# A window-attention block with MLP on one core: finer waits and another order at the start of the MLP stage

## What is computed

```python
y = layernorm(x, g1, b1); y = roll(y, (-2, -2))
# windows of 4 x 32 = 128 tokens, 16 per image, 4 heads of 8 channels
q, k, v = split(xw @ qkv_w + qkv_b)
attn = softmax(q * SCALE @ k.T + bias + mask)
o = (attn @ v) @ proj_w + proj_b
x = x + roll(o, (2, 2))
z = layernorm(x, g2, b2)
z = gelu(z @ fc1_w + fc1_b) @ fc2_w + fc2_b      # 32 -> 128 -> 32 channels, exact Gelu
return x + z
```

## Time and profile before

| | us |
|---|---|
| median of 3 runs | 214.05 |
| lowest and highest | 213.61, 214.38 |
| the profiled execution | 213.55 |
| its span in the profile | 211.7 |
| TensorE busy | 190.5 (90%) |
| VectorE busy | 157.1 (74%) |
| ScalarE busy | 146.6 (69%) |
| GpSimd busy | 134.1 (63%) |

### The profile page before, as it was taken

How to read it: one execution, slowest core, us unless ns; L and a number is a source line. 1 busy time by engine, 2 the same in 40 slices (tenths; PEclk the granted TensorE clock), 3 DMA queues, 4 the chain that set the end, 5 groups by cost and what they waited for, 6 DMA issues and landing times.

```text
span 211.7 us, 10978 instructions
## 1 busy us (share of the span) xinstructions
PE 190.5 (90%) x4768; PEld 115.9 (55%) x4768; DVE 157.1 (74%) x221; ACT 146.6 (69%) x217; POOL 134.1 (63%) x148
## 2 busy tenths in 40 slices
PE   0789869798989999999999999999999998979884
PEld 0754534456556657656665676576567654443212
DVE  3895956675768878876987888687766977657874
ACT  7555378645868588768867895877557656588883
POOL 7786399671246995999499869844762291702730
PEclk9999979999999999999999999999999999999999
DMA  6924538656433741554365236414620000000324
GB/s 187 273 65 143 172 125 246 165 174 191 137 119 105 217 141 60 176 155 132 107 182 161 81 112 177 127 62 152 207 58 5 8 5 6 3 0 3 150 99 152
DMA packets 24296, 25.61 MB, mean 121 GB/s; under 512 B 3556, under 2 KB 21732, under 8 KB 24164
## 3 DMA queue, kind: packets, MB, share of 16 engines
q1 hardware_dynamic: 23496, 24.16, 37.3%
q10 hardware_dynamic: 752, 0.74, 1.3%
HBM read 16.24 MB, written 8.39 MB: 116 GB/s over the span
## 4 chain that ended last, share of the span: by engine, by line
PE 53%; POOL 13%; issue 13%; ACT 7%; SPq 5%; DVE 4%; DMA 3%; POOLq 0%; DVEq 0%; ACTq 0%
PE pav L992 10%; PE ps L957 9%; PE ps L972 7%; POOL rstd L403 4%; SPq L213 4%; PE ps L943 4%; PE ps L919 4%; PE ps L1010 3%; POOL parts L421 3%; PE pq L1094 3%; PE pq L880 2%; PE pq L1100 2%; ACT prob L765 2%; DMA X<-x_tok 2%; ACT q_rows L770 2%
## 5 line engine op out<-in xcount | busy, mean ns | idle before, releaser
L560 DVE TENSOR_REDUCE m_parts<-ps 128x8 f32<-128x1024 f32 x64 | 78.1, 1222 | 31.7 <-PE ps L943 31.4
L765 ACT ACTIVATE prob<-ps 128x1024 f32<-128x1024 f32 x64 | 65.5, 1024 | 34.9 <-PE ps L972 33.6
L403 POOL TENSOR_TENSOR rstd<-var,neghalf 128x16 f32<-128x16 f32 x16 | 47.4, 2963 | 8.2 <-DVE var L525 7.3
L992 PE MATMUL pav<-prob,va 128*32 128x128 f32 x1024 | 42.2, 278 | 0.2 <-issue 0.2
L957 PE MATMUL ps<-rel_j,id_b 96*32 96x512 bf16 x512 | 40.2, 380 | 2.2 <-DVE m_parts L560 0.9
L972 PEld LDWEIGHTS ps<-q_rows,k_rows 64*64 64x64 bf16 x1024 | 16.9, 106 | 27.0 <-issue 22.4
L992 PEld LDWEIGHTS pav<-prob,va 128*32 128x32 f32 x1024 | 24.8, 109 | 9.5 <-ACT prob L765 4.6
L972 PE MATMUL ps<-q_rows,k_rows 64*64 64x128 bf16 x1024 | 27.6, 224 | 1.8 <-DMA q_rows<-m_rows 1.6
L943 PEld LDWEIGHTS ps<-k_rows,q_rows 64*64 64x64 bf16 x1024 | 22.7, 108 | 6.5 <-issue 0.6
L943 PE MATMUL ps<-k_rows,q_rows 64*64 64x128 bf16 x1024 | 25.6, 217 | 0.0
L919 PE MATMUL ps<-rel_i,ident_b 64*64 64x512 bf16 x256 | 25.3, 383 | 0.0
(11 more groups left out here) (128 smaller groups left out, 309.4 us busy)
## 6 DMA issues: line engine op xcount, KB each, us to landing
slots<-parts SPq DMA_DIRECT2D x21, 256.0 KB, 3.0
q_rows<-slots SPq DMA_DIRECT2D x42, 128.0 KB
k_rows<-slots SPq DMA_DIRECT2D x40, 128.0 KB
X<-x_tok SPq DMA_DIRECT2D x8, 256.0 KB, 4.0
y_tok<-res SPq DMA_DIRECT2D x7, 256.0 KB, 2.0
q_rows<-m_rows SPq DMA_DIRECT2D x32, 8.0 KB
bias_parts<-rel_parts SPq DMA_DIRECT2D x3, 128.0 KB
slots<-parts SPq DMA_DIRECT2D x3, 128.0 KB, 3.5
```

Of the source, the lines that this page charges most:

```text
L403: pool.tensor_tensor(rstd[:, i, :], var[:, i, :], neghalf[:], ALU.pow).then_inc(rstd_done[i], 1)
L560: dve.tensor_reduce(dst, first_home(j)[:].rearrange("p (a u n) -> p a u n", u=2, n=TOK), AX.X, ALU.max, negate=True).then_inc(max_done, 1)
L765: act.activation(prob[:, j % NPROB, :], ps2[:], ACT.Exp).then_inc(exp_done, 1)
L992: mm = pe.matmul(pav[32 * h:32 * (h + 1), 128 * (j % 4):128 * (j % 4 + 1)], va[:, b % 2, at:at + 32], prob[:, j % NPROB, src:src + 128], s ...
```

## The change

`fc1` gets a parameter `halves`. The wait for older Gelus now stands ahead of each half: half h of image m waits for 2m + h - 2 finished Gelu halves (0 or less is no wait). The waits that only guard the first call stand as before. At the start of the end stage, half 0 of `fc1(1)` stands ahead of `tokens_first(15)`, half 1 behind it; `fc1(2)` and `project_out(15)` stand ahead of `fc2(0)`, which `fc2(1)` follows directly. On VectorE, `add_attention(15)` stands ahead of `mlp_tokens(0)`.

```diff
--- before.py
+++ after.py
@@ -698,8 +698,8 @@
             copy_oT(OCTETS - 1)
             normalize(OCTETS - 1)
             copy_onT(OCTETS - 1)
+            add_attention(OCTETS - 1)
             mlp_tokens(0)
-            add_attention(OCTETS - 1)
             dve.wait_ge(x2_done, OCTETS)
             means(second_norm(B - 1), B - 1)
             center(second_norm(B - 1), B - 1)
@@ -994,23 +994,23 @@
                                        start=wi == 0, stop=wi == 1)
                 mm.then_inc(av_done, 1)
 
-            def fc1(m):
-                pe.wait_ge(yT2_done, m + 1)
+            def fc1(m, halves=(0, 1)):
+                if 0 in halves:
+                    pe.wait_ge(yT2_done, m + 1)
                 if m == 0:
                     pe.wait_ge(max_done, PAIRS)
                     pe.wait_ge(mrow_done, GROUPS)
                     pe.wait_ge(va_done, B)
                     pe.wait_ge(x2_done, OCTETS - 2)
-                else:
-                    pe.wait_ge(gelu_done, 2 * m - 1)
-                if m == 1:
-                    pe.wait_ge(exp_done, PAIRS)
-                for wx in range(GW):
-                    bank = FC1[(2 * m + wx // 2) % 3][:, 512 * (wx % 2):512 * (wx % 2 + 1)]
-                    mm = pe.matmul(bank, w1[32 * wx:32 * (wx + 1), :], yT2[32 * wx:32 * (wx + 1), m, :], start=True,
-                                   stop=True)
-                    if wx % 2 == 1:
-                        mm.then_inc(fc1_done, 1)
+                for half in halves:
+                    if m == 1 and half == 0:
+                        pe.wait_ge(exp_done, PAIRS)
+                    after(pe, gelu_done, 2 * m + half - 2)
+                    for wx in (2 * half, 2 * half + 1):
+                        bank = FC1[(2 * m + half) % 3][:, 512 * (wx % 2):512 * (wx % 2 + 1)]
+                        mm = pe.matmul(bank, w1[32 * wx:32 * (wx + 1), :], yT2[32 * wx:32 * (wx + 1), m, :],
+                                       start=True, stop=True)
+                    mm.then_inc(fc1_done, 1)
 
             def fc2_last():
                 pe.wait_ge(xT_done, 1)
@@ -1188,12 +1188,13 @@
             project_out(OCTETS - 2)
             weighted_values(PAIRS - 2)
             weighted_values(PAIRS - 1)
+            fc1(1, (0,))
             tokens_first(OCTETS - 1)
-            fc1(1)
+            fc1(1, (1,))
             channels_first(OCTETS - 1)
+            fc1(2)
+            project_out(OCTETS - 1)
             fc2(0)
-            project_out(OCTETS - 1)
-            fc1(2)
             fc2(1)
             for m in range(3, B):
                 fc1(m)
```

## The result

| | before | the change |
|---|---|---|
| median of 22 runs each, us | 214.02 | 215.74 |
| lowest and highest | 212.83, 215.85 | 213.45, 219.55 |
| ratio, 95% interval | | 1.0065 (1.004 to 1.009) |
| the profiled execution | 213.55 | 213.45 |
| its span | 211.7 | 211.0 |

What follows compares the result with a forecast made beforehand. TensorE and ScalarE bound the end stage at 2.43 us an image, VectorE close behind. Pitch gain and transition loss cancel; VectorE's delay adds 1.37 us at L1018 to the 214.05 median, giving 215.4 us, range 214.4 to 216.3.

Steps and rivals of the forecast that it cites:

- The pitch: TensorE and ScalarE loop over images: half waits give 2.25 us an image instead of 2.43, about 0.7 us from fc1(3) to fc1(7).
- the range's lower corner: Lower bound: if half an fc1 costs 0.53 us, project_out and all behind it come 0.54 earlier, leaving +0.83 us.
- The transition: Start of the end stage on TensorE: the new order starts fc2(0) at 193.16 instead of 190.81, 2.35 us later.
- The VectorE term: VectorE's in-order queue: late fc2(0) delays image 7's sums by 1.98 us, xT to 207.97 and L1018 by 1.37 us.
- Everything in it is moved alike: VectorE and GpSimd, image 7's sums to yT2(7): a fixed chain of 8.88 us, shifted whole, putting yT2(7) at 203.87.
- the slack before xT: VectorE before L1018 in the kernel before: xT could end 0.18 us later, counting 0.05 us from VectorE's end to TensorE's start.
- The output wait: Last transposes, about 209.85: their buffer is free by 207.4 + 2.0, or 2.4 at most, so no second delay.
- A: Rival on TensorE: fc1's passes keep strict order, three passes, 2.60 us an image, L1018 +1.49, 215.5 us; chance 0.07.
- B: Rival on TensorE: a gated half does not overlap the other, 3.13 us an image, +4.6, 218.6 us; chance 0.05.
- C: Rival: no change, the late fc2(0) does not reach the end or freed halves wait anyway, 214.0 us; chance 0.09.
- D: Rival: faster, the pitch decides with no loss at the transition, 5 x 0.18 = 0.9 us, 213.2 us; chance 0.05.

Runs made afterwards that it cites:

- e2: The change, but both halves of fc1 wait for the younger Gelu again from image 2 on; ratio 1.0043 to the kernel before.
- e1: The kernel before with only the half waits added, in the old order; ratio 0.9960 to the kernel before.
- e9: The change with fc2(0) and the projection put back ahead of fc1(2), the rest kept; ratio 0.9965 to the kernel before.
- e10: e9 with VectorE's old order too, mlp_tokens(0) ahead of add_attention(15); ratio 0.9939 to the kernel before.
- e3: The change with image 7's sums, mean and centering moved ahead of mlp_tokens(0) on VectorE; ratio 0.9996 to the kernel before.
- e4: The change with xT one pair of token transpose and residual earlier on VectorE; ratio 1.0055 to the kernel before.
- e5: e4 with the last two transposes writing a buffer of their own; ratio 1.0063 to the kernel before.
- e6: The kernel before with half waits, xT one pair earlier and an own buffer for the last transposes; ratio 0.9963, repeated 0.9985.
- e8: e6 without the half waits, so the kernel before with earlier xT and the own buffer; ratio 1.0037 to the kernel before.

## Why the prediction was right

It forecast 215.4 us, 0.64% over the 214.05 of its time. Measured are 215.74 and a ratio of 1.0065. By the trace the mechanism is the one forecast: a late fc2(0) makes the norm of image 7 late, and that delay reaches the end. The end stage got 1.13 us longer where 1.37 was forecast. That the time moved by 1.39 us, even nearer to 1.37, is in part luck: its interval is 0.9 to 1.9 us.

**The pitch**, the time from one image to the next. Forecast 2.25 us instead of 2.43; measured 2.20 and 2.43. The 0.05 comes from one term: the gate, the time from a Gelu's start to the half fc1 that waits for its end, was taken as 1.26 us from a whole fc1, and a second half starts after 1.17 (196.85 to 198.02). With it two images take 1.17 (fc1 to its Gelu) + 1.17 (the gate) + 1.07 (half an fc1) + 0.99 (fc2) = 4.40. Half an fc1 alone was put at 1.07, between 0.53 and 1.07; measured 1.05 and 1.06. That took the range's lower corner away. It was decided by reading the row for what repeats (two passes) and not for how many products there are.

**The transition.** Up to fc2(0) all steps came within 0.13 us: fc2(0) moved by 2.22 us, forecast 2.35. Most of the difference is the same gate, 1.17 us from gelu(1,0) to fc1(2)'s second half (188.40 to 189.57). In e2, where fc1(2) waits whole at the same place, it is 1.25. So the half that follows on is quicker than a whole one; why, no run shows. Behind it fc2(1) came 0.89 us after fc2(0), not 0.99. Thus fc2(6), forecast at 19.26 from t0 and level with before, starts at 18.95, 0.36 ahead of before (19.31): on TensorE gain and loss didn't quite cancel, which nobody sees at the end, because L1018 waits for xT.

**The VectorE term.** Forecast +1.98 for the sums, measured +1.80; forecast +1.37 for L1018, measured +1.15. The 0.22 add up from the forecast's own steps: the sums 0.18 earlier, the chain from them to yT2(7) 8.64 instead of the 8.88 taken as fixed, 0.24 less, then 0.10 and 0.10 more. Of the 0.24, GpSimd's scaling makes up 0.20 (1.15 us at 200.49 instead of 1.35). "Everything in it is moved alike" was not quite so. The unbroken work behind yT2(7), forecast 4.10 us, measured 205.88 - 201.68 = 4.20: m_tok(5) follows res(4) by 0.80 (203.02 to 203.82), where 1.13 less the wait of 0.43 had been taken. And L1018 follows xT's end by 0.15, not 0.05 (e1: 206.45 to 206.60), so that the slack before xT in the kernel before was 0.08 and not 0.18. Errors of both signs in part cancelled.

**Does the chain set the end?** e1, e9 and e10 confirm it by undoing parts: with fc2(0) and the sums earlier, the end came earlier. But the prediction named xT as the place at which the delay reaches the end, as if it were the only one. e3 and e4 showed that moving the sums or xT alone gains little or nothing, and e5 that the queue behind yT2(7) bounds the end even where xT is early. In the prediction's step the sum is the same, because xT stands near the queue's end; as advice on what to move it would have misled, as it did in my expectations of e3 and e4.

**The output wait**, passed in the prediction "if narrowly", didn't bind in the change, but it was undersized: in e4 the last transposes started 2.77 us behind the end of res(5) (208.56 to 211.33), where 2.0, or 2.4 at most, had been counted. By the forecast's own times, 207.4 + 2.77 = 210.2 against 209.85, it would have held them up by 0.3 us.

**The rivals.** A fell: the second half of fc1(5) starts at 198.02, ahead of the first half's second pass at 198.28, and the pitch is 2.20, not 2.60. The Trainium skill ("TensorE: Matmul & The Clock Gate", The mechanism) has matmuls start in strict program order; the trace does not agree with that for the two passes of fp32 products on separate rows, since 198.28 belongs to the product that is earlier in the program. B fell with it: 0.27 us apart, two halves end 1.06 behind the second. C fell by the result. D, the pitch alone, is what e1 and e10 are, and they are faster, by 0.4 and 0.6%; the change is not, because it carries the order with it.

## What to carry to other kernels

When an instruction is moved behind others on one engine, follow its first consumer, and count the whole queue of that consumer's engine up to the end of the kernel, not only the one instruction that shows as a wait. If that queue holds a step of another engine, as image 7's norm does with GpSimd's, follow the step too. Take a gain at one engine only as far as the next engine's slack reaches: the half waits had 1.07 us to give at L1018 (20.31 to 19.24, e6), VectorE let 0.67 of them through in the old order (19.64, e1) and none in the new. Test the parts apart: one half of this change is 0.4% faster alone, and the other half turned it into a loss.

## What the runs showed of the hardware

The granted clock of TensorE falls in the opening stretch of some executions and not of others. In the profile of before it is 0.50, the lower of the two levels (1.2 GHz), from 29 to 32 us, behind a microsecond (28 to 29) in which TensorE was busy for 0.05 us. In that of the change it stays at 1.00 from 26 to 37 us, though TensorE was busy for only 0.01 us from 28 to 29. The dip doesn't explain the spans: at octet 0, at 46 us, the two executions are 0.10 us apart. What makes them differ by 1.65 us more up to octet 12, at a clock of 1.00 in both, stays unexplained, as does this: 213.45 and 216.43 us are two executions of the change at clock 1.0.

Products on separate row groups of the array overlapped at the distances in time that occurred, 0.27 us for fc1(5) and 0.59 us for fc1(2), and a half of them costs as much as all.

GpSimd's elementwise work is not of fixed length, and what it takes goes with how long a `res` of VectorE, started before it, still runs beside it. The scaling took 1.35 us before and 1.36 in e8, where res(3) ran beside it for 0.44 and 0.45 us, and 1.15 in the change and in e3, where it did so for 0.25 and 0.24. The square took 1.42 before and in the change, with res(0) beside it for 0.53 and 0.51. All of these are 0.9 us and the overlap. In e3 the square started first and took 1.04, and res(0) took 1.00 instead of 0.69. So a VectorE that waits for TensorE can lengthen a step on GpSimd: before, m_tok(3) waited 0.30 us for fc2(3), res(3) came later and the scaling got longer. No run was made to test this by itself. These are the rows of before, VectorE's two and GpSimd's one:

```profile
199.51 0.72 DVE L584 STREAM_TRANSPOSE m_tok<-pq 128x512 f32<-128x512 f32 x1 [0.30 <-PE pq L1040]
200.26 0.69 DVE L590 TENSOR_TENSOR res<-m_tok,X 128x512 f32<-128x512 f32 x1
200.51 1.35 POOL L413 TENSOR_TENSOR yn<-xc,rstd 128x512 f32<-128x512 f32 x1
```
